# Cross attention and experts on one core: 192 key slots a batch, queries made half a period earlier, the first batch's rows on VectorE, four score banks before the first logits

## The chip, the cores and the metric

One core of one Trainium2 chip. The metric is the device time of one execution in microseconds, the median of several runs. One execution was also profiled; the rows below are of that one.

## What is computed

Eight batches of 512 tokens, width 256. Cut to what matters:

```python
x  = x + tanh(g_xattn) * xattn(layernorm(x), ctx)          # (8, 512, 256)
x  = x + tanh(g_ffn)   * experts(layernorm(x))

def xattn(q, kv):
    qp = q @ Wq.T
    idx = argmax(qp @ kv.T, -1)                 # each token picks ONE of 512 context rows
    mkv = take(kv, idx) @ Wkv.T                 # 512 picked rows, many of them the same
    mk, mv = split(mkv)                         # one head of width 16, shared by 16 query heads
    out = softmax(heads(qp) @ mk.T / 4) @ mv
    return out @ Wc.T

def experts(x):                                 # 8 experts, the best 2 of each token
    ...gelu(x @ w1[e] + b1[e]) @ w2[e] + b2[e]
```

The kernel does not attend to 512 picked rows but to the distinct ones, each with the number of tokens that picked it. It packs them into a fixed number of slots (`SLOTS`). Each batch's number of distinct rows is kept in `k.n_chosen`; where one exceeds `SLOTS`, a flag (`k.wide`) sends all engines through a second, general path that does select and attend again over 512 keys. Counted from the reference on its inputs, the eight batches pick 164, 173, 168, 148, 161, 148, 171 and 167 distinct rows.

## The kernel before

`flow` handles all batches in one software pipeline. `each_step` runs through periods `p` and 32 steps in each; every engine's program is written out in this order, and an engine keeps it strictly. In period `p` the kernel attends for batch `p` (logits, exponentials, weighted values), takes the row maxima of batch `p + 1`, selects keys for batch `s = p + 2`, and finishes batch `e = p - 1` (heads, output projection, residual, second layernorm, gate, expert queues). A table of constants (`PE_TURN_X`, `ACT_QUERY`, `DVE_QUEUE` and so on) says at which step of a period an engine issues a piece of work. No real time passes in a step that holds no work.

What is written in each period, by engine, with the names and lines of the profile:

- **TensorE.** `turn_x` (L980) turns the normalised rows at step 0, `project` (L997) makes the queries at steps 2 and 3, `keys_values` (L1007), four `scores` (L1022) at steps 5, 7, 9 and 11, `counts` (L1032) at 15, `ranks` (L1040) at 18, `pack` (L1048, L1052) at 22. One `logits_b` (L1065, two products of 256 columns) a step makes the logits from which VectorE takes row maxima; its first tile for a batch comes `MAX_EARLY` = 7 steps before the period of that work. One `logits` (L1086) a step, `weighted` (L1096) every fourth. For the batch before: `turn_heads`, `project_out` (L1121), `turn_rows`, `gates`, `rank` (L1152) at step 30.
- **VectorE.** `take_max` (L815) once a step, `best_key` (L784, L785) after each of the four scores, `x_stats` (L844), `positions` (L802 is its scan), and at steps 29 to 31 `choose`, `shares` (L900 to L906) and `queue_slots` (L911 to L918).
- **ScalarE.** `exponentials` (L677) once a step, copies out of PSUM (`turned_x`, `query`, `copy_sums` L683 at lag 11), `packed_keys` (L654).
- **GpSimd.** `chosen_keys` (L547, L548), `places` (L564), `normalise_x` (L573), `query_lo` (L541), weight remainders (L616), and `scatter` (L592), eight indirect DMAs, at step 31.
- **SyncE.** `queries` stores the split queries and loads them again in another layout; `load_x`, `load_ctx`, `load_piece` (weights).

Three banks matter for waits. Scores and `logits_b` share the two banks `ps_d` in turn; `logits` has the two banks `ps_a`, which stay unused until batch 0's first logits; `ps_r` and `ps_e` are shared by most small products. Before use, TensorE waits until the last reader of the bank is done.

```python
def max_tile(p, step):
    m, tile = divmod(p * STEPS + step + MAX_EARLY, STEPS)
    return (m + 1, tile) if is_batch(m + 1) else None
...
bank_d[n % 2].wait_read(pe)
```

After `flow`, `experts` (L2166 on) runs 39 tiles of 256 queued rows with TensorE without a break.

## Time and profile before

| | us |
|---|---|
| median of 3 runs | 1034.34 (1034.08 to 1035.05) |
| the profiled execution | 1032.27 |
| its span in the trace | 1030.5 |
| start of batch 0's first logits | 103.61 |
| starts of periods 1 to 7 | 155.2, 208.6, 265.3, 322.3, 379.3, 436.2, 481.2 |
| end of period 7 | 520.8 |
| first product of the expert tiles | 587.42 |

TensorE is busy 847.4 us of the span (82%), VectorE 546.3 (53%), GpSimd 456.3 (44%), ScalarE 410.3 (40%). How to read the rows of the timeline further down: start, length, engine, line, operation, output tile and input tiles, shape, how many instructions are merged (x8); in square brackets how long the engine had been idle before and what ended that. TensorE's instructions overlap, so what one costs is the distance between starts. A float32 product shows as two records.

### The profile page before, as it was taken

The numbers are of one execution on the slowest core, as the hardware profiler recorded it, in microseconds if no ns is written. First come the engines' busy times: TensorE is split into PE (matmuls) and PEld (weight loads), VectorE is DVE, ScalarE is ACT, GpSimd is POOL, SyncE is SP. The second block draws the span as 40 slices with busy tenths as digits, with TensorE's granted clock in tenths as the row PEclk, the third lists the DMA queues.
The fourth block names the chain that finished last, engine by engine and source line by source line (L and its number), as shares of the span: only waits on it lengthen the run. The fifth ranks groups of instructions, "written<-read, shape, count | busy, mean of one in ns | idle before, by whom it ended". The sixth has DMA issues, their size and how long they took to land. (4 is left out here: it accounts for less than half of the span.)

```text
span 1030.5 us, 20778 instructions
## 1 busy us (share of the span) xinstructions
PE 847.4 (82%) x6444; PEld 583.5 (57%) x6445; DVE 546.3 (53%) x1518; ACT 410.3 (40%) x818; POOL 456.3 (44%) x491
## 2 busy tenths in 40 slices
PE   2486889888887879787741199999999999999994
PEld 1232334444343434332230189889998898898884
DVE  2457486867686775865133144544545545445441
ACT  1120354645455453657631043433333334334330
POOL 6857263656555565443454012333423323323334
PEclk9776899989999989989975599999999999999998
DMA  4523414243342424222432422231322322322310
GB/s 154 133 91 84 87 48 92 84 123 94 101 96 94 109 68 83 83 100 83 129 102 92 131 42 43 42 50 32 56 44 41 57 43 41 60 42 41 53 14 2
DMA packets 65691, 76.40 MB, mean 74 GB/s; under 512 B 7392, under 2 KB 59360, under 8 KB 65504
## 3 DMA queue, kind: packets, MB, share of 16 engines
q1 hardware_dynamic: 51328, 58.74, 21.4%
q0 software_dynamic: 14304, 16.93, 9.3%
q8 instruction: 30, 0.49, 0.2%
q14 instruction: 29, 0.24, 0.1%
HBM read 47.68 MB, written 29.53 MB: 75 GB/s over the span
## 5 line engine op out<-in xcount | busy, mean ns | idle before, releaser
L677 ACT ACTIVATE prob<-ps_a 128x512 f32<-128x512 f32 x256 | 151.5, 602 | 190.3 <-PE ps_a L1086 184.5
L815 DVE TENSOR_REDUCE row_max<-ps_d 128x2 f32<-128x512 f32 x256 | 170.0, 682 | 85.7 <-PE ps_d L1065 78.5
L2340 PE MATMUL ps_h<-x_hi,w_split 128*128 128x256 bf16 x1248 | 212.2, 274 | 0.0
L2354 PE MATMUL ps_y<-w_split,hidden 128*128 x1248 | 206.4, 273 | 0.0
L2340 PE MATMUL ps_h<-x_lo,w_split 128*128 128x256 bf16 x624 | 170.8, 274 | 0.0
L2354 PE MATMUL ps_y<-w_split,h_lo 128*128 x624 | 170.1, 273 | 0.0
L2250 ACT ACTIVATE hidden<-ps_h,bias 128x256 f32<-128x256 f32 x312 | 130.8, 470 | 88.3 <-PE ps_h L2340 88.3
L2224 POOL DMA_INDIRECT out<-y,token_at x78 | 129.3, 1657 | 43.9 <-POOL token_at L2222 30.5
L1065 PE MATMUL ps_d<-k_st,w_split 96*128 96x256 bf16 x512 | 107.1, 296 | 32.9 <-DVE row_max L815 20.9
L2340 PEld LDWEIGHTS ps_h<-x_hi,w_split 128*128 x1248 | 122.6, 98 | 14.3
L2354 PEld LDWEIGHTS ps_y<-w_split,hidden 128*128 128x128 bf16 x1248 | 122.1, 98 | 14.1
L2220 POOL TENSOR_TENSOR token_f<-tails,ones_f 128x2 f32<-128x2 f32 x39 | 7.8, 200 | 267.2 <-DVE y L2296 266.0
L2293 DVE TENSOR_TENSOR y<-ps_y,b_all 128x512 f32<-128x512 f32 x39 | 27.0, 691 | 174.6 <-PE ps_y L2354 174.6
L2239 ACT CAST x_hi<-ps_x 128x512 bf16<-128x512 f32 x39 | 22.8, 585 | 212.1 <-PE ps_x L2327 212.1
L1086 PE MATMUL ps_a<-w_split,k_st 98*128 98x512 bf16 x256 | 100.4, 398 | 7.9 <-ACT prob L677 6.6
L2307 DVE TENSOR_TENSOR h_lo<-hidden 128x512 bf16<-128x512 f32 x156 | 99.6, 683 | 12.3 <-ACT hidden L2250 9.4
L616 POOL TENSOR_TENSOR w_split<-w_stage,w_split 128x1024 bf16<-128x1024 f32 x32 | 68.0, 2129 | 85.6 <-ACT w_split L746 85.5
L1065 PEld LDWEIGHTS ps_d<-k_st,w_split 96*128 96x128 bf16 x512 | 45.5, 102 | 101.7 <-DVE row_max L815 44.5
L1096 PE MATMUL ps_o<-prob,v_st 128*32 128x512 f32 x512 | 72.0, 636 | 0.7 <-ACT prob L677 0.7
L592 POOL DMA_INDIRECT queue<-rows,slot x64 | 62.9, 982 | 19.4 <-issue 17.1
L1086 PEld LDWEIGHTS ps_a<-w_split,k_st 98*128 98x128 bf16 x256 | 24.8, 99 | 74.3 <-ACT prob L677 48.3
L1022 PE MATMUL ps_d<-ctx_sb,q_t 128*128 128x512 f32 x128 | 62.3, 611 | 4.2 <-DVE row_max L815 3.5
(190 smaller groups left out, 1078.1 us busy)
## 6 DMA issues: line engine op xcount, KB each, us to landing
w_stage<-w SPq DMA_DIRECT2D x32, 512.0 KB, 3.4
xg<-queue SPq DMA_DIRECT2D x39, 260.0 KB
w_split<-q_split SPq DMA_DIRECT2D x24, 256.0 KB, 6.4
x_in<-x SPq DMA_DIRECT2D x8, 512.0 KB
ctx_sb<-ctx_t SPq DMA_DIRECT2D x8, 512.0 KB, 3.5
x<-x SPq DMA_DIRECT2D x8, 512.0 KB, 3.4
q_split<-q_hl SPq DMA_DIRECT2D x16, 256.0 KB, 2.3
out<-x SPq DMA_DIRECT2D x8, 512.0 KB, 3.0
```

What stands on the lines that cost most here:

```text
L592: pool.indirect_dma_start(k.queue[:], bass.IndirectOffsetOnAxis(ap=slot[:, t, c:c + 1], axis=0), rows[:, t, :], None).then_inc(scattered, 16)
L616: g.tensor_tensor(lo, stage, hi, ALU.subtract).then_inc(w_lo, 1)
L677: a.activation(prob[n % 2][:, j, :], ps_a[step % 2][:], ACT.Exp, scale=SCALE).then_inc(exp_ready, 1)
L815: v.tensor_reduce(row_max[:, t, 2 * pair:2 * pair + 2], bank.rearrange("p (h r) -> p h r", h=2), AX.X, ALU.max).then_inc(max_taken, 1)
L1065: last = t_.matmul(ps_d[n % 2][:, c * SLOTS:(c + 1) * SLOTS], q_st[m % 3][0:ROW_MAX, 2 * pair + c, t * P:(t + 1) * P], k_st[0:ROW_MAX, m % ...
L1086: t_.matmul(ps_a[step % 2][:], k_st[:, b % 3, key_tile * P:(key_tile + 1) * P], q_st[b % 3][:, QUAD * group + j, :], start=True, stop=True ...
L1096: last = t_.matmul(ps_o[j * VW:(j + 1) * VW, :], v_st[:, b % 3, key_tile, :], prob[n % 2][:, j, :], start=(key_tile == 0), stop=(key_tile ...
L2224: pool.indirect_dma_start(k.out_rows, bass.IndirectOffsetOnAxis(ap=token_at[:, t:t + 1], axis=0), y[s][:, t, :], None, bounds_check=B * L ...
L2250: last = a.activation(hidden[s][:, f, :], ps_h[n][:, c, :], ACT.Gelu, bias=bias[s][:, f:f + 1])
L2307: v.tensor_tensor(h_lo[s][:, both, :], hidden[s][:, both, :], h_hi[s][:, both, :], ALU.subtract).then_inc(h_lo_ready, 1)
L2340: last = t_.matmul(ps_h[n][:, c, :], k.w1_split[:, bass.ds(e, 1), part, kt, f].rearrange("p a f -> p (a f)"), xs[s][:, kt, :], start=(q == ...
L2354: last = t_.matmul(ps_y[s][:, t, :], hs[s][:, f, token], k.w2_split[:, bass.ds(e, 1), part, f, :].rearrange("p a d -> p (a d)"), start=(q ...
```

## The change

Seven edits, all in `flow`:

1. `SLOTS` is 192 instead of 256. `logits_b` multiplies 2 x 192 columns, `take_max` reduces 384 elements instead of 512, `places` compares with 192 columns. The second key tile holds 64 keys: for two heads at a time two products of 64 rows go to the upper and lower half of one bank, and one exponential reads both. A group of four heads has 6 banks of logits instead of 8, at steps 0, 1, 2, 3, 4 and 6 of eight (`LOGITS_AT`). `packed_keys` copies the values in three pieces, not one, and `pack` has 24 value products, not 16.
2. `turn_x` and `project` for a batch move from steps 0, 2, 3 of period `s - 2` to steps 14, 16, 17 of period `s - 3`; with them the copies on ScalarE, the remainders on GpSimd (step 24) and the store on SyncE (step 25). The reload (`stack`) stays in period `s - 2`, at step 1. Loading and normalising x move a period earlier too.
3. Batch 0's `normalise_x`, `chosen_keys` and `places` are done by VectorE; for the other batches GpSimd keeps them.
4. In periods before 0, scores and `logits_b` go round four banks (`ps_d` and `ps_a`).
5. `rank` moves from step 30 to 31, `queue_slots` and `scatter` from step 31 to step 0 of the period after.
6. `copy_sums` has lag 10, not 11.
7. New waits: `turned_x` waits for `project_out` of the batch four before, `turned_rows` for the `project` of the batch four later, since they share the tile `turned`.

```diff
-SLOTS = SLOT_TILES * P
+SLOTS = 192
...
+        FEW = SLOTS - P
+        LOGITS_AT = (0, 1, 2, 3, 4, 6)
...
-        PE_TURN_X, PE_PROJECT, PE_KV, PE_TURN_KV, PE_SCORES = 0, (2, 3), 6, 8, (5, 7, 9, 11)
+        PE_TURN_X, PE_PROJECT, PE_KV, PE_TURN_KV, PE_SCORES = 14, (16, 17), 6, 8, (5, 7, 9, 11)
...
+        def ring(p, n):
+
+            return n % 4 if p < 0 else n % 2
...
+                if s == 0:
+                    dve.wait_ge(scores_read, t + 1)
+                    chain.then(v.tensor_copy(best[:, t:t + 1], top8_at[:, t, 0:1]))
+                    v.tensor_scalar(chosen[:, t, :], column[:], best[:, t:t + 1], None, ALU.is_equal
+                                    ).then_inc(chosen_ready, 1)
...
+                if s == 0:
+                    dve.wait_ge(position_ready, 1)
+                    for t in range(LT):
+                        last = v.tensor_scalar(place[:, t, :], column[:, 0:SLOTS], position[:, t:t + 1], None, ALU.is_equal)
+                    last.then_inc(place_ready, 1)
...
+                if i < QUAD:
+                    last = t_.matmul(ps_a[i % 2][:], k_st[:, b % 3, 0:P], q_st[b % 3][:, QUAD * group + i, :],
+                                     start=True, stop=True)
+                else:
+                    for c in range(2):
+                        last = t_.matmul(ps_a[i % 2][c * FEW:(c + 1) * FEW, :], k_st[:, b % 3, P:SLOTS],
+                                         q_st[b % 3][:, QUAD * group + 2 * (i - QUAD) + c, :], start=True, stop=True)
```

What the tables move, first on TensorE before the first packing (`ps_e<-ident,x_in` is `turn_x`, `ps_e<-turned,wq_sb` `project`, `ps_r<-ones_bf,chosen` `counts`, `ps_r<-used,...` `ranks`, `ps_e<-chosen,key_cols` the start of `pack`). Before:

```order
L1022 MATMUL ps_d<-ctx_sb,q_t 128x512 x4
L1032 MATMUL ps_r<-ones_bf,chosen 128x1 x16
L1040 MATMUL ps_r<-used,before 128x4
L1041 MATMUL ps_r<-used,ones_bf 128x4
L1048 MATMUL ps_e<-chosen,key_cols 98x256 x4
```

With the change:

```order
L1064 MATMUL ps_a0<-ctx_sb,q_t 128x512 x2
L1064 MATMUL ps_a1<-ctx_sb,q_t 128x512 x2
L1022 MATMUL ps_e0<-ident,x_in 128x128 x4
L1022 MATMUL ps_e1<-ident,x_in 128x128 x4
L1074 MATMUL ps_r<-ones_bf,chosen 128x1 x16
L1039 MATMUL ps_e0<-turned,wq_sb 128x512 x2
L1039 MATMUL ps_e1<-turned,wq_sb 128x512 x2
L1082 MATMUL ps_r<-used,before 128x4
L1083 MATMUL ps_r<-used,ones_bf 128x4
L1090 MATMUL ps_e0<-chosen,key_cols 98x192 x4
```

The turn and the projection of batch 1 now stand inside batch 0's selection, the projection ahead of its ranks; the last scores use the banks `ps_a`.

Then on TensorE at the border of two periods in the middle of the run (`ps_r<-either,...` is `rank`, `ps_o<-prob,v_st` `weighted`). Before:

```order
L1086 MATMUL ps_a<-w_split,k_st 128x512
L1065 MATMUL ps_d<-k_st,w_split 128x256 x2
L1152 MATMUL ps_r<-either,before 128x32
L1153 MATMUL ps_r<-either,ones_bf 128x32
L1086 MATMUL ps_a<-w_split,k_st 128x512
L1065 MATMUL ps_d<-k_st,w_split 128x256 x2
L1086 MATMUL ps_a<-w_split,k_st 128x512
L1065 MATMUL ps_d<-k_st,w_split 128x256 x2
L980 MATMUL ps_e<-ident,x_in 128x128 x8
```

With the change:

```order
L1131 MATMUL ps_a<-w_split,k_st 64x512 x2
L1107 MATMUL ps_d<-k_st,w_split 128x192 x4
L1200 MATMUL ps_r<-either,before 128x32
L1201 MATMUL ps_r<-either,ones_bf 128x32
L1127 MATMUL ps_a<-w_split,k_st 128x512
L1107 MATMUL ps_d<-k_st,w_split 128x192 x2
L1127 MATMUL ps_a<-w_split,k_st 128x512
L1107 MATMUL ps_d<-k_st,w_split 128x192 x2
L1144 MATMUL ps_o<-prob,v_st 32x512 x4
```

`turn_x` and, behind it, the projection are gone from here; one step more of row-maximum products stands ahead of `rank`.

And on VectorE at the same border (`row_max` rows are `take_max`, `rows<-share,ratio` and `token` end `shares`, `queue_end` begins `queue_slots`). Before:

```order
L905 TENSOR_TENSOR rows<-share,ratio 128x4
L906 TENSOR_SCALAR token<-token 128x4
L911 TENSOR_TENSOR queue_end<-n_queued,queue_at 128x8
L914 TENSOR_TENSOR queue_end<-queue_end,ps_r 128x8
L915 TENSOR_TENSOR n_queued<-n_queued,ps_r 128x8
```

With the change:

```order
L946 TENSOR_TENSOR rows<-share,ratio 128x4
L947 TENSOR_SCALAR token<-token 128x4
L849 TENSOR_REDUCE row_max<-ps_d 128x2
L58 ISA
L952 TENSOR_TENSOR queue_end<-n_queued,queue_at 128x8
L955 TENSOR_TENSOR queue_end<-queue_end,ps_r 128x8
```

One row maximum stands between the two pieces now; the pieces are the same.

## Rows read from the trace of the kernel before

**Rows 1.** Page, the chain that ended last, by line.

```profile
PE ps_h L2340 20%; PE ps_y L2354 19%; PE ps_x L2327 2%; DMA xg<-queue 1%; DMA out<-y,token_at 0%; POOL out L2224 0%; DVE y L2293 0%; DVE x_lo L2285 0%; ACT x_hi L2239 0%; DVEq L2181 0%; SPq L2152 0%; SPq L2195 0%; SPq L2191 0%; DVE y L2296 0%; POOL token_f L2220 0%
```

**Rows 2.** Stretches: length; PE, PEld, DVE, ACT, POOL busy; clock, DMA share, GB/s.

```profile
103.61:155.18 51.57, 44.51 (x258) 19.59 (x259) 33.49 (x74) 24.71 (x46) 24.06 (x25) 0.91 0.29 68
...
322.34:379.32 56.98, 46.99 (x321) 23.22 (x320) 41.21 (x124) 29.94 (x57) 33.59 (x37) 1.00 0.37 98
...
436.20:481.20 45.00, 36.27 (x222) 16.00 (x220) 28.98 (x88) 27.73 (x50) 18.04 (x16) 0.89 0.31 104
481.20:520.80 39.60, 28.21 (x170) 11.03 (x170) 11.41 (x62) 27.96 (x52) 17.97 (x16) 0.96 0.34 110
520.80:576.60 55.80, 13.62 (x63) 9.38 (x63) 15.65 (x79) 8.94 (x15) 26.29 (x26) 0.57 0.32 105
```

**Rows 3.** Timeline of TensorE ahead of period 0.

```profile
49.62 1.09 PE L1048 MATMUL ps_e<-chosen,key_cols 128*98 128x256 bf16 x4 [6.95 <-POOL chosen L564]
60.23 3.75 PE L997 MATMUL ps_e<-turned,wq_sb 128*128 128x512 f32 x4 [0.40 <-ACT turned L635]
67.49 1.96 PE L1022 MATMUL ps_d<-ctx_sb,q_t 128*128 128x512 f32 x4 [0.66 <-DVE row_max L815]
94.98 1.09 PE L1048 MATMUL ps_e<-chosen,key_cols 128*98 128x256 bf16 x4 [1.59 <-POOL chosen L564]
103.61 0.61 PE L1086 MATMUL ps_a<-w_split,k_st 98*128 98x512 bf16 x1 [0.50 <-DMA w_split<-max_t]
```

**Rows 4.** Timeline of VectorE and GpSimd ahead of period 0.

```profile
9.39 1.41 DVE L844 BATCH_NORM_STATS2 stats<-x_in 128x6 f32<-128x256 f32 x4
28.81 0.70 DVE L784 MAX8 top<-ps_d 128x8 f32<-128x512 f32 x1 [17.60 <-PE ps_d L1022]
43.55 2.09 DVE L802 TENSOR_TENSOR_SCAN offset<-ones_f,total 128x4 f32<-128x4 f32 x1
...
12.79 4.83 POOL L573 TENSOR_SCALAR x_in<-x_in,moments,rstd 128x256 f32<-128x256 f32 x4
39.70 1.57 POOL L548 TENSOR_SCALAR chosen<-column,best 128x512 bf16<-128x512 f16 x1
43.50 2.12 POOL L616 TENSOR_TENSOR w_split<-w_stage,w_split 128x1024 bf16<-128x1024 f32 x1
45.94 3.62 POOL L564 TENSOR_SCALAR chosen<-column,position 128x256 bf16<-128x256 f16 x4 [0.32 <-DVE position L803]
```

**Rows 5.** Timeline of TensorE in period 4 and at its end.

```profile
325.74 0.39 PE L1065 MATMUL ps_d<-k_st,w_split 96*128 96x256 bf16 x2 [2.14 <-DVE row_max L815]
...
327.06 0.39 PE L1086 MATMUL ps_a<-w_split,k_st 98*128 98x512 bf16 x1
327.29 0.39 PE L1065 MATMUL ps_d<-k_st,w_split 96*128 96x256 bf16 x2
327.51 1.88 PE L997 MATMUL ps_e<-turned,wq_sb 128*128 128x512 f32 x4
...
357.15 0.39 PE L1086 MATMUL ps_a<-w_split,k_st 98*128 98x512 bf16 x1 [0.62 <-ACT prob L677]
361.12 0.39 PE L1065 MATMUL ps_d<-k_st,w_split 96*128 96x256 bf16 x2 [0.64 <-DVE row_max L815]
365.39 0.64 PE L1048 MATMUL ps_e<-chosen,key_cols 128*98 128x256 bf16 x4 [1.15 <-POOL chosen L564]
373.26 0.66 PE L1105 MATMUL ps_r<-ident,sums 128*128 128x128 f32 x4 [0.51 <-ACT sums L683]
377.72 0.19 PE L1152 MATMUL ps_r<-either,before 128*128 128x32 bf16 x1 [1.72 <-DVE either L896]
```

**Rows 6.** Timeline of VectorE in period 4: three row maxima in a run.

```profile
324.99 1.89 DVE L815 TENSOR_REDUCE row_max<-ps_d 128x2 f32<-128x512 f32 x3
```

**Rows 7.** Timeline of TensorE around step 1 of period 6.

```profile
441.38 1.94 PE L1096 MATMUL ps_o<-prob,v_st 128*32 128x512 f32 x8
447.48 1.07 PE L1096 MATMUL ps_o<-prob,v_st 128*32 128x512 f32 x8
```

More of the change, by code:

```diff
@@ L282, in flow @@
         max_t = sb(own, "max_t", [2 * H, L], BF16)
-        prob = [sb(own, f"prob{c}", [P, QUAD, L]) for c in range(2)]
+        prob = [sb(own, f"prob{c}", [P, QUAD // (c + 1), L]) for c in range(2)]
         sums = sb(own, "sums", [P, L])
@@ L488, in _ @@
                 m, s, e = p + 1, p + 2, p - 1
-                if step == SP_X and p > -3 and is_batch(p + 3):
-                    load_x(p + 3)
-                if step == SP_QUERIES and is_batch(s):
-                    queries(s)
+                if step == SP_X and p > -4 and is_batch(p + 4):
+                    load_x(p + 4)
+                if step == SP_QUERIES and is_batch(p + 3):
+                    queries(p + 3)
+                if step == SP_STACK and is_batch(s):
+                    stack(s)
                 if step == SP_CTX and is_batch(s) and is_batch(s + 1):
@@ L557, in values @@
                 chain.then(g.tensor_copy(value_cols[:, :, 0:V1], value_f[:]))
-                chain.step(g.tensor_tensor(value_cols[:, :, V1:2 * V1], value_f[:], value_cols[:, :, 0:V1], ALU.subtract))
+                last = g.tensor_tensor(value_cols[:, :, V1:2 * V1], value_f[:], value_cols[:, :, 0:V1], ALU.subtract)
+                if s:
+                    chain.step(last)
+                else:
+                    last.then_inc(place_ready, 1)
             def places(s):
@@ L596, in _ @@
                 s, e = p + 2, p - 1
-                if step == POOL_QUERY_LO and is_batch(s):
-                    query_lo(s)
-                for t in due(s, POOL_CHOSEN, step):
+                if step == POOL_QUERY_LO and is_batch(p + 3):
+                    query_lo(p + 3)
+                for t in (due(s, POOL_CHOSEN, step) if s else ()):
                     chosen_keys(s, t)
@@ L931, in _ @@
                 if step in DVE_BEST and is_batch(s):
-                    best_key(s, DVE_BEST.index(step), ps_d[n_d % 2][:])
+                    best_key(s, DVE_BEST.index(step), (ps_d + ps_a)[ring(p, n_d)][:])
                     n_d += 1
@@ L935, in _ @@
                     add(e, c)
-                for t in due(p + 3, DVE_X_STATS, step):
-                    x_stats(p + 3, t)
+                for t in due(p + 4, DVE_X_STATS, step):
+                    x_stats(p + 4, t)
                 for t in due(e, DVE_STATS, step):
@@ L947, in _ @@
                     shift_of(e)
[L948 to L949 removed]
+                if step == DVE_X_MOMENTS and is_batch(p + 4):
+                    x_moments_of(p + 4)
                 if step == DVE_SPLIT_MAX and is_batch(m):
@@ L957, in _ @@
                     shares(e)
-                if step == DVE_QUEUE and is_batch(e):
-                    queue_slots(e)
+                if step == DVE_QUEUE and is_batch(e - 1):
+                    queue_slots(e - 1)
                 row_tile = max_tile(p, step)
                 if row_tile:
-                    take_max(*row_tile, ps_d[n_d % 2][:])
+                    take_max(*row_tile, (ps_d + ps_a)[ring(p, n_d)][:])
                     n_d += 1
@@ L1159, in _ @@
                 if is_batch(p):
-                    logits(p, step)
+                    if step % (2 * QUAD) in LOGITS_AT:
+                        logits(p, step // (2 * QUAD), LOGITS_AT.index(step % (2 * QUAD)))
                 row_tile = max_tile(p, step)
                 if row_tile:
-                    logits_b(*row_tile, n_d)
+                    logits_b(*row_tile, ring(p, n_d))
                     n_d += 1
@@ L1170, in _ @@
                     turn_sums(*given)
-                if step == PE_TURN_X and is_batch(s):
-                    turn_x(s)
-                if step in PE_PROJECT and is_batch(s):
-                    project(s, PE_PROJECT.index(step))
+                if step == PE_TURN_X and is_batch(p + 3):
+                    turn_x(p + 3)
+                if step in PE_PROJECT and is_batch(p + 3):
+                    project(p + 3, PE_PROJECT.index(step))
                 if step == PE_KV and is_batch(s):
@@ L1181, in _ @@
                 if step in PE_SCORES and is_batch(s):
-                    scores(s, PE_SCORES.index(step), n_d)
+                    scores(s, PE_SCORES.index(step), ring(p, n_d))
                     n_d += 1
```

142 lines of the change are left out of this document (80 added, 62 removed).

## The prediction

> **What bounds the kernel now.** I read the chain that ended last first. It reaches back only to 577 us, and what stands in it is TensorE in the two layers of the experts [rows 1], a stage that the change does not touch: it gives and costs nothing, if the expert tiles merely start earlier. So the whole effect is the time at which `flow` ends. The busy time by stretch [rows 2] splits that: period 0 takes 51.6 us, period 4 57.0 (periods 2 to 5 are 56.7 to 57.0, period 1 is 53.4), period 6 45.0, period 7 39.6, then a tail of 55.8 without attention. In period 4 TensorE is busy 47.0 of 57.0 us and VectorE 41.2: TensorE bounds it, with waits on VectorE. Ahead of period 0 it is another picture: 103.6 us in which TensorE mostly waits for one serial chain through VectorE and GpSimd [rows 3, 4]. Durations are those of the profiled execution, 1032.27 us; the median of the runs is 2.1 us above it. An effect under 0.2% (2 us) could not be told from none.
>
> **Unit costs.** A row maximum over 512 elements comes every 0.60 us in a run (1.89 for three, the last one 0.69 long) [rows 6]; statistics over 256 elements come every 0.35 [rows 4]. Between them 384 elements cost 0.47. On GpSimd 512 columns take 1.57 us and 256 take 0.90 (3.62 for four) [rows 4], so 192 take 0.74. On TensorE one logits product takes 0.23 from start to start, a pair for the row maxima 0.22, that is 0.11 for 256 columns, so 0.08 for 192; half a projection takes about 1.72 (1.88 with its overlap) [rows 5].
>
> **1. Up to the first packing (49.6 us now).** Normalising batch 0 on GpSimd takes 4.83 us [rows 4]; on VectorE four instructions of 256 elements, 0.35 each by the nearest row, 1.4: the chain starts 3.4 earlier, the first `best_key` at 25.4 instead of 28.8. On VectorE each tile then costs 1.45 for maximum and index, 0.2 for the copy and at most 0.6 for the comparison, with keys and values (0.8) 9.8 us in all: the last row of batch 0 is chosen at 35.3, while GpSimd ends at 41.3 now (39.70 plus 1.57 [rows 4]). That would be 6 us. Two things take most of it back. First, the order: batch 1's projection stands ahead of batch 0's `ranks`. Its input is normalised by GpSimd only after `query_lo` of batch 0 (until 26.4), 1.3 us of deviation and 4.83: 32.6; turned and copied at about 36. The projection takes 3.4 us at the full clock and 7.1 at half (3.75 is one half of it at the low clock [rows 3]); I take 6: ranks at about 43, later than the 42.5 of now. Second, VectorE and GpSimd get in each other's way: the scan over five elements takes 2.09 us and ends at 45.64, when GpSimd's weight remainder, begun at 43.50, ends at 45.62 [rows 4]. Copies and comparisons of batch 0 on VectorE would wait so behind `query_lo`, four normalisations of 1.2 and the remainders, about 3 us in all, and positions come 3.3 us behind the ranks. The Trainium skill's page "SBUF — State Buffer" (section "SBUF: two separate sides") has the rule: GpSimd and VectorE share one pair of ports and the loser waits for the whole instruction, if VectorE reads two SBUF inputs or is in a two-port mode. By this row it holds for the scan; by the page it would also hold for VectorE's new comparisons, and for these no row exists: without it this part would be 3 us better. The place comparisons take 4 x 0.35 instead of 3.62. Sum: first packing at about 48.5, **-1**, bounds -3.5 (no collision, projection at full clock) and +2 (every new VectorE instruction waits behind one of GpSimd).
>
> **2. From there to the first logits (54.0 us now, 49.62 to 103.61).** Four parts. Up to the first scores of batch 1 (67.49 [rows 3]) TensorE has 12 tiles of row maxima with `turn_x` and a projection at the low clock in between; afterwards 12 tiles from four banks at VectorE's 0.47: 5.9 instead of 15.6, -9.7. The four scores and eight tiles took 17.4 us, each score and each maximum waiting for the other through two banks; with four, VectorE's own work is the bound, 4 x 1.45 + 8 x 0.47 + 0.8 = 10.4, and the first score runs at the low clock: 12, -5. Turn and projection of batch 2 are new at steps 14 to 17: +3.6. The places take 0.7 less, and nothing but them and positions stands between ranks and pack (94.98): -1.6. From pack to logits it is the same chain, 8.6 us. Sum -12.7, I take **-12**; bounds -18 (full clock throughout) and -5 (all of TensorE's work in it at half clock).
>
> **3. Period 0 (51.6).** Steps 0 to 4 lose turn and projection, which ran at the low clock: 12.8 us become 5.7, -7.1. The same work returns at steps 14 to 17, 2 x 1.72 + 0.9 and 0.5 of waiting for its copy, +4.9; the first scores fall to the low clock, +1.8. Products for the maxima -1.7 (64 x 0.027), waits -1.9. **-4**.
>
> **4. Periods 1 to 4.** The products give -1.7 each, where TensorE bounds. The waits at steps 15 to 18, 0.62 on an exponential, 0.28 and 0.64 on row maxima, go under the projection that now stands there: -1.5 [rows 5]. The wait of 0.51 on `copy_sums` goes with its lag: -0.5. At the border of the periods VectorE's `choose` (2.95), `shares` (1.1) and `queue_slots` (1.9) stay, only cut in two, with five row maxima 8.4 us, in which TensorE has 3.8 us of work; the waits of 1.72 and 2.14 [rows 5] are not removed but moved, and grow to about 4.5, since turn and projection no longer fill this place. Up to the start of step 3 this stretch takes 1.6 less than now, but the turn's 0.9 is paid elsewhere: -0.75. What is late next: `pack` waits for the places (1.15 now [rows 5]), about 1.6, as TensorE has less to do before: +0.45. Turn and projection at their new place wait 0.2 for `add` and 0.5 for their copy: +0.7; scores wait 0.2 more. `pack` has eight small products more, +0.1. Logits: 6 banks, but 8 products as before, four of them in pairs of 64 rows; I count them at the full 0.23 each and no gain. ScalarE's eight exponentials a period fewer (0.5 each) cost nothing and give nothing here; it is busy 29.9 of 57. `scatter` and `stack` have moved past GpSimd's and SyncE's other work; GpSimd's first `chosen_keys` comes 3 us later than VectorE's result, and catches up by the third, as each takes 1.75 and they come every 4.2. Sum **-3.0** in each of 2, 3 and 4, -2.5 in period 1; bounds -6 and 0.
>
> **5. Period 5** also loses a turn and a projection (4.3), as batch 7 is projected in period 4, and gets 1.3 of the waits back that the projection had covered: **-6**. **Period 6** (45.0): products -1.7, sums -1.6, row maxima -0.7: **-4**. **Period 7** (39.6) goes from exponential to exponential through two banks, 0.54 each: two fewer in each of four groups, -4.3; pairs +0.8; sums one exponential earlier, -2.5: **-6**. **Tail**: it hangs on GpSimd, which must end the scatter of batch 6 before the weight remainders and the last deviation; `queue_slots` and `scatter` come as soon as before, as no step with work lies in between: 0.
>
> Sum: -1 - 12 - 4 - 2.5 - 9 - 6 - 4 - 6 = **-44.5**. From the median of 1034.3 that is **990**; the profile's own time would be 988.
>
> **The rivals.** *A. Paired halves (chance 0.15).* Four products with 32 columns, 8 records, take 1.07 us together [rows 7], while two full float32 products take over 1.8 (1.96, [rows 3]): narrow products run side by side. If the 64-row pairs do, each pair takes 0.23 and not 0.46, 8 x 0.23 = 1.8 a period, 14 in all: about 976. Against it: a pair of row-maximum products just before a change to narrow ones costs 0.1 more than elsewhere, and there are eight changes a period more. The page "TensorEngine Tiling (Array Packing)" of the Trainium skill says both: up to twice as fast for 64 columns ("Theoretical Speedup"), and a drain of the array at each change of mode ("Key Properties"); by the first 976, by the second again 990. *B. VectorE bounds the border and gives nothing to the steady periods (0.13).* Then only parts 1 to 3 and the ends remain, with 4.3 in period 5: -1 - 12 - 4 - 4.3 - 2 - 4 = -27, 1007. For it: the waits of 1.72 and 2.14 grow. *C. The lead loses more (0.12).* The lock and the projection ahead of the ranks cost what the four banks give: parts 1 and 2 together -4, 999. *D. The clock (0.04), slower.* At the border TensorE now idles over half of 8.4 us with no projection behind it. In period 6, which already is so, `weighted` takes 1.94 at 441.4 and 1.07 again at 447.5 [rows 7]: the clock fell to half (1.2 GHz) and came back within 6 us. Should it stay low in periods 1 to 5 through steps 30 to 13, some 18 us of work would double: +90 against -44.5, 1080. It decides from 9 us a period on; period 6 speaks against it, with at most 3. *E. The change doesn't do what it says (0.01):* a batch with more than 192 rows would send all through the general path, select and attend again, +400 (the length of periods 0 to 7). The largest count is 173.
>
> **How the numbers follow.** Forecast 0.55, A 0.15, B 0.13, C 0.12, D 0.04, E 0.01. The forecast's own bounds with A's below and B's above give 974 to 1008, which leaves out D, E and the ends of A and B, under 0.2. Faster by over 0.2%: 0.93, as A, B, C and the forecast all are, less what I may have missed; the same 0.02; slower 0.05.
>
> **What would show it.** First logits at about 90.5 (now 103.6), first packing near 48.5, batch 1's projection before it. Row maxima 0.47 apart in a run. Period 0 near 47.5, periods 2 to 4 near 54, 5 near 51, 6 near 41, 7 near 33.5; end of period 7 near 476, tail still 56. Waits on `row_max` at steps 1 and 2 of 1 to 2 us each, none at 15 to 18. I am wrong if the first packing comes after 52, if periods 2 to 4 are still 57, or if `weighted` in steps 29 to 9 of the middle periods takes 1.9.

## The result and the profile after

The changed kernel takes 994.03 us (median of 4 runs, 993.29 to 994.43), the kernel before 1034.62 beside it: ratio 0.9612, 95% interval 0.9596 to 0.9628. That is 40.6 us, where 44.5 were forecast; 994 lies inside 974 to 1008. The profiled execution took 994.43 us, its span is 992.7 us. Runs more than 1.5% above the fastest of their kernel are left out of the ratios further down, but not of the medians and ranges: two of `border_undone`, one of `all_three`. The sum came out nearly right, its parts did not. `rank` is issued once near the end of each period from 1 on, so its starts cut the run into comparable pieces:

| stretch | before | after | difference | forecast |
|---|---|---|---|---|
| start of the span to first packing | 49.62 | 52.90 | +3.3 | -1 |
| first packing to first logits | 53.99 | 47.07 | -6.9 | -12 |
| first logits to first `rank` (periods 0, 1) | 103.41 | 94.76 | -8.7 | -6.5 |
| next three (periods 2, 3, 4) | 56.88, 57.02, 56.80 | 55.88, 52.08, 54.91 | -1.0, -4.9, -1.9 | -3 each |
| period 5 | 58.30 | 49.99 | -8.3 | -6 |
| period 6 | 45.06 | 36.42 | -8.6 | -4 |
| period 7 | 38.56 | 35.41 | -3.2 | -6 |
| to the last `rank` | 33.54 | 33.83 | +0.3 | 0 |
| to the first product of the expert tiles | 34.24 | 35.76 | +1.5 | 0 |

The page of after, the chain that ended last, by line. It is the chain of [rows 1], link by link; the two largest shares are a point higher, of a span that is 37.8 us shorter:

```profile
PE ps_h L2389 21%; PE ps_y L2403 20%; PE ps_x L2376 2%; DMA xg<-queue 1%; DMA out<-y,token_at 0%; POOL out L2273 0%; DVE y L2342 0%; DVE x_lo L2334 0%; ACT x_hi L2288 0%; DVEq L2230 0%; SPq L2201 0%; SPq L2244 0%; SPq L2240 0%; DVE y L2345 0%; POOL token_f L2269 0%
```

So the whole difference is again when the expert tiles start: 549.01 instead of 587.42 us.

Timeline of TensorE after, the lead (`ps_e<-chosen,key_cols` starts a packing, L1127 is batch 0's first logits):

```profile
52.90 0.87 PE L1090 MATMUL ps_e<-chosen,key_cols 128*98 128x192 bf16 x4 [9.53 <-DVE chosen L836]
55.71 0.80 PE L1107 MATMUL ps_d<-k_st,w_split 96*128 96x192 bf16 x4 [0.95 <-issue]
61.11 3.75 PE L1064 MATMUL ps_d<-ctx_sb,q_t 128*128 128x512 f32 x4
73.78 1.04 PE L1022 MATMUL ps_e<-ident,x_in 128*128 128x128 f32 x8
78.47 0.56 PE L1074 MATMUL ps_r<-ones_bf,chosen 128*128 128x1 bf16 x16 [3.12 <-POOL chosen L559]
79.17 3.41 PE L1039 MATMUL ps_e<-turned,wq_sb 128*128 128x512 f32 x4
91.27 0.88 PE L1090 MATMUL ps_e<-chosen,key_cols 128*98 128x192 bf16 x4 [5.62 <-POOL chosen L579]
99.97 0.61 PE L1127 MATMUL ps_a<-w_split,k_st 98*128 98x512 bf16 x1 [2.14 <-DMA w_split<-max_t]
```

Timeline of VectorE ahead of the first packing:

```profile
38.51 1.15 DVE L821 TENSOR_SCALAR used<-count 128x4 bf16<-128x4 f32 x1
...
50.84 0.43 DVE L878 BATCH_NORM_STATS2 stats<-x_in 128x6 f32<-128x256 f32 x1 [10.98 <-DMA x_in<-x]
51.37 0.16 DVE L828 TENSOR_TENSOR position<-ps_r,unused 128x4 f32<-128x4 f32 x1
...
52.04 0.81 DVE L836 TENSOR_SCALAR chosen<-column,position 128x192 bf16<-128x192 f16 x4
```

Two things are to be seen. Up to the first packing VectorE stands idle for 10.98 us, not for batch 0's ranks, which had been ready since 43.4, but for a load of x that batch 2 needs: its first statistics stand at step 18, and `positions` of batch 0 at step 19 behind them. From 55.71 to 73.78 the second selection goes nearly as forecast (5.4 us to the first scores and 12.7 through them, forecast 5.9 and 12). Then it takes 17.5 to the second packing, with 3.12 and 5.62 us of waiting for GpSimd; my terms give 12.1 there (10.1 before, +3.6, -1.6).

The stretches between `rank`s after (length; PE, PEld, DVE, ACT, POOL busy; clock, DMA share, GB/s):

```profile
194.73:250.61 55.88, 50.52 (x328) 24.58 (x327) 37.55 (x123) 25.57 (x50) 33.05 (x37) 0.88 0.39 100
250.61:302.69 52.08, 46.12 (x329) 22.53 (x327) 37.34 (x123) 25.27 (x50) 32.83 (x37) 0.97 0.42 108
302.69:357.60 54.91, 49.02 (x329) 23.59 (x328) 36.06 (x115) 25.38 (x50) 26.81 (x31) 0.91 0.38 92
357.60:407.59 49.99, 43.10 (x312) 20.80 (x311) 36.56 (x117) 22.79 (x45) 24.69 (x30) 0.92 0.35 83
407.59:444.01 36.42, 31.94 (x219) 14.68 (x216) 24.52 (x87) 23.16 (x42) 18.02 (x16) 0.92 0.36 114
444.01:479.42 35.41, 28.42 (x163) 11.37 (x164) 10.58 (x57) 23.10 (x43) 17.95 (x16) 0.86 0.37 120
```

The first three hold the same work and differ by 3.8 us; the longer, the lower the granted clock (0.88, 0.91, 0.97). Before, the same three stood at 0.94, 0.97 and 1.00 and were alike to 0.2 us, so there the low clock cost nothing. TensorE behind the border, after:

```profile
194.56 0.34 PE L1107 MATMUL ps_d<-k_st,w_split 96*128 96x192 bf16 x2 [2.56 <-DVE row_max L849]
194.73 0.18 PE L1200 MATMUL ps_r<-either,before 128*128 128x32 bf16 x1
...
196.58 0.50 PE L1107 MATMUL ps_d<-k_st,w_split 96*128 96x192 bf16 x2 [0.46 <-DVE row_max L849]
197.01 1.94 PE L1144 MATMUL ps_o<-prob,v_st 128*32 128x512 f32 x8
...
202.66 1.94 PE L1144 MATMUL ps_o<-prob,v_st 128*32 128x512 f32 x8
```

`weighted` takes 1.94, as in the first of [rows 7]: the clock has fallen to 1.2 GHz, the lower of its two levels, and `weighted` is at it still at 202.66. In the middle stretch only one `weighted` is so. The first stretch has a second time at 1.2 GHz, from 239 to 243 in the middle of its period, with no wait over 0.46 us just before it. VectorE and GpSimd in the wait at the border, after:

```profile
192.12 1.27 DVE L931 TENSOR_TENSOR gap<-top 128x4 f32<-128x4 f32 x1
...
193.51 0.17 DVE L934 COPY rows<-choice 128x4 f32<-128x4 f32 x1
```

```profile
191.25 2.12 POOL L635 TENSOR_TENSOR w_split<-w_stage,w_split 128x1024 bf16<-128x1024 f32 x1
```

A subtraction of four columns takes 1.27 us and ends with GpSimd's instruction; a copy of as many takes 0.17.

### The profile page after: what moved, and what is told of

It reads as the page before. It is cut to its first block and busy times, and to the rows that moved or that the text cites. A ratio compares the mean times of both kernels' runs of the same rounds, so it can differ in the third digit from the quotient of the medians.

```text
span 992.7 us, 20863 instructions
## 1 busy us (share of the span) xinstructions
PE 832.3 (84%) x6508; PEld 579.8 (58%) x6509; DVE 517.9 (52%) x1534; ACT 376.7 (38%) x770; POOL 438.1 (44%) x475
## 5 line engine op out<-in xcount | busy, mean ns | idle before, releaser
L698 ACT ACTIVATE prob<-ps_a 128x512 f32<-128x512 f32 x192 | 113.0, 603 | 181.5 <-PE ps_a L1127 108.2
L849 DVE TENSOR_REDUCE row_max<-ps_d 128x2 f32<-128x384 f32 x237 | 127.9, 551 | 60.8 <-PE ps_d L1107 59.2
L1107 PE MATMUL ps_d<-k_st,w_split 96*128 96x192 bf16 x474 | 84.5, 268 | 25.7 <-DVE row_max L849 19.2
L1107 PEld LDWEIGHTS ps_d<-k_st,w_split 96*128 96x128 bf16 x474 | 40.0, 103 | 77.6 <-DVE row_max L849 32.0
L1144 PE MATMUL ps_o<-prob,v_st 128*32 128x512 f32 x512 | 77.1, 678 | 3.0 <-ACT prob L698 3.0
L2389 PEld LDWEIGHTS ps_h<-x_lo,w_split 128*128 x624 | 61.4, 98 | 7.4
L2403 PEld LDWEIGHTS ps_y<-w_split,h_lo 128*128 128x128 bf16 x624 | 61.1, 98 | 7.1
L1064 PE MATMUL ps_d<-ctx_sb,q_t 128*128 128x512 f32 x112 | 57.8, 640 | 2.2 <-DVE row_max L849 1.4
```

The source lines that it names most:

```text
L698: a.activation(prob[n % 2][:, j, :], ps_a[i % 2][:], ACT.Exp, scale=SCALE).then_inc(exp_ready, 1)
L849: v.tensor_reduce(row_max[:, t, 2 * pair:2 * pair + 2], bank[:, 0:2 * SLOTS].rearrange("p (h r) -> p h r", h=2), AX.X, ALU.max).then_inc(m ...
L1064: last = t_.matmul(ps_da[n][:], q_t[:, kt, t * P:(t + 1) * P], ctx_sb[:, kt, :], start=(kt == 0), stop=(kt == KT - 1))
L1107: last = t_.matmul(ps_da[n][:, c * SLOTS:(c + 1) * SLOTS], q_st[m % 3][0:ROW_MAX, 2 * pair + c, t * P:(t + 1) * P], k_st[0:ROW_MAX, m % 3, ...
L1144: last = t_.matmul(ps_o[j * VW:(j + 1) * VW, :], values, probs, start=(key_tile == 0), stop=(key_tile == SLOT_TILES - 1))
L2389: last = t_.matmul(ps_h[n][:, c, :], k.w1_split[:, bass.ds(e, 1), part, kt, f].rearrange("p a f -> p (a f)"), xs[s][:, kt, :], start=(q == ...
```

## The experiments

Medians in us; a difference between two of these kernels is uncertain by about 3 us, and by 4 to 6 where one of them is `filler`, `all_three` or `border_undone`, whose runs spread more. "Pack" and "logits" are the starts of the first packing and of batch 0's first logits in the profiled execution.

| kernel | median (lowest to highest) | ratio to before, 95% | pack | logits |
|---|---|---|---|---|
| the change | 994.03 (993.29 to 994.43) | 0.9596 to 0.9628 | 52.90 | 99.97 |
| `slots_only` | 1011.86 (1009.52 to 1017.69) | 0.9765 to 0.9823 | 51.48 | 102.98 |
| `stats_after` | 986.74 (985.84 to 988.10) | 0.9534 to 0.9574 | 45.19 | 93.66 |
| `rows_pool` | 1004.38 (1001.92 to 1004.89) | 0.9688 to 0.9732 | 62.83 | 109.89 |
| `two_banks` | 993.20 (990.16 to 996.00) | 0.9583 to 0.9627 | 51.48 | 103.41 |
| `banks_late` | 991.88 (988.73 to 993.93) | 0.9560 to 0.9611 | 47.31 | 101.81 |
| `project_late` | 971.54 (970.46 to 976.61) | 0.9387 to 0.9437 | 46.64 | 88.53 |
| `border_undone` | 1002.38 (994.82 to 1014.72) | 0.9621 to 0.9728 | 50.19 | 98.08 |
| `sums_late` | 1003.70 (999.83 to 1005.21) | 0.9688 to 0.9737 | 51.02 | 97.62 |
| `weights_moved` | 982.05 (979.73 to 983.90) | 0.9482 to 0.9527 | 49.80 | 96.81 |
| `filler` | 983.11 (981.18 to 994.33) | 0.9493 to 0.9569 | 53.85 | 100.79 |
| `best` | 976.00 (973.70 to 977.00) | 0.9419 to 0.9462 | 45.02 | 91.01 |
| `all_three` | 973.51 (966.60 to 983.96) | 0.9372 to 0.9446 | 46.60 | 89.29 |

**The slots alone.** All places that edit 1 touches, in the kernel before:

```diff
-SLOTS = SLOT_TILES * P
+SLOTS = 192
```

> Edit: the kernel before with 192 slots alone (edit 1); turn and projection, banks, batch 0's rows, `rank`, `queue_slots` and `copy_sums` as before. Theory (my terms of the sum, with the pairs of 64 rows at the 0.34 that the change's trace shows): row maxima of the lead -3, period 0 -2, periods 1 to 5 -2 each, period 6 -2.5, period 7 -4: about -21, 1013, ratio 0.980. Rival 1 (the moves make room for it, alone it goes into waits on row maxima and exponentials): -10, 1024, ratio 0.990. Rival 2 (nearly all of the gain is this edit): -33 or more, 1001, ratio below 0.97.

1011.86, 22 us under before: the theory's 21. Its profiled execution took 1015.10. Between its `rank`s it takes 54.97, 54.80, 56.32, 54.69, 43.47 and 37.42. The edit is worth half of the change, and 1.9, 2.2 and 0.5 us in the middle periods; against this kernel the moves took 2.7 and 1.4 off two of the middle periods and added 0.9 to one, and took 4.7 and 7.1 off periods 5 and 6.

**The load of x.**

```diff
-DVE_X_STATS, DVE_X_MOMENTS = (18, 22, 22, 23), 24
+DVE_X_STATS, DVE_X_MOMENTS = (20, 22, 22, 23), 24
```

> Edit: the first tile of the x statistics goes from step 18 to step 20, behind `positions` on VectorE. Theory (the load of x): in the change, VectorE stands 10.98 us in front of this tile while the ranks of batch 0 are ready behind it; without that, the first packing comes at 45 to 46 us instead of 52.9, the first logits at about 92.5 instead of 99.97, and the time is 986 to 987 (ratio to before 0.954). Rival 1 (projection and ports, as I forecast them): the chain of ranks, positions and places is itself not ready before about 50; first packing 50 or later, time 991 to 993. Rival 2: the gain is taken back by the first logits, which wait for loads anyway: 993 to 994.

986.74. TensorE of this kernel:

```profile
36.84 6.74 PE L1039 MATMUL ps_e<-turned,wq_sb 128*128 128x512 f32 x8
43.42 0.17 PE L1082 MATMUL ps_r<-used,before 128*128 128x4 bf16 x1
...
45.19 0.53 PE L1090 MATMUL ps_e<-chosen,key_cols 128*98 128x192 bf16 x4 [1.57 <-DVE chosen L836]
```

The packing comes 1.8 us behind the ranks, and 6.3 of the 7.7 gained there reach the first logits. Another 2.7 come in the first middle stretch (53.22 us, with one `weighted` at the low clock instead of two, and no second fall in the middle of the period), and 0.6 are lost in periods 0 and 1. One number of a step in a table cost the change 7 us.

**Batch 0's rows (edit 3).** The copy, comparison, places and normalisation of batch 0 go back to GpSimd, with their semaphores; the diff is shortened:

```diff
-for t in (due(s, POOL_CHOSEN, step) if s else ()):
+for t in due(s, POOL_CHOSEN, step):
...
-if step == POOL_PLACE and is_batch(s) and s:
+if step == POOL_PLACE and is_batch(s):
...
```

> Edit 3 undone alone: batch 0's normalisation, chosen keys and places on GpSimd again. Theory (VectorE waits for the load of x at the same place, and that load hangs on the store and reload of batch 0's queries, which come 3.4 us later): first packing at 58 to 59 instead of 52.9 (3 from the later load, 2.8 from the places), time about 999. Rival 1 (all of it lies beside the wait for the load, but for the places): +3, 997. Rival 2 (GpSimd without these pieces helped only itself): 994.

1004.38, more than forecast. GpSimd of this kernel:

```profile
48.08 1.58 POOL L559 TENSOR_SCALAR chosen<-column,best 128x512 bf16<-128x512 f16 x1
...
57.68 2.12 POOL L629 TENSOR_TENSOR w_split<-w_stage,w_split 128x1024 bf16<-128x1024 f32 x1 [5.75 <-ACT w_split L764]
59.78 2.99 POOL L576 TENSOR_SCALAR chosen<-column,position 128x192 bf16<-128x192 f16 x4
```

Batch 0's last keys are chosen at 49.7 instead of 37.6, so the load of x (landed by 53.1) no longer decides alone, and the places stand behind a weight remainder that waits for ScalarE. Edit 3 is worth 10 us here; I had put -1 on all of part 1. But 49.7 is also 8.4 later than in the kernel before (41.3), since GpSimd now normalises batch 1 (33.41 to 38.26) ahead of batch 0's chosen keys: in part edit 3 pays back what edit 2 costs. Edit 2 was not undone by itself in any run, so its own worth stays open. The edits that were measured alone, 22 us for the slots, 10 for this one, 5 for the four banks and 10 for the sums (both below), already come to more than the 40.6 of the whole; whether they add isn't shown.

**The four banks (edit 4)**, first on the change, then on `stats_after`:

```diff
-return n % 4 if p < 0 else n % 2
+return n % 2
```

> Edit: in the periods before 0 scores and row-maximum logits go round two banks again, not four. Theory (my forecast of 5 us for the four banks): first packing unchanged at 52.9, first logits at 105, time 998 to 999. Rival: the lead goes at the pace of VectorE and GpSimd, and two banks do as well: 994 to 995.

> Two banks again in the periods before 0, as in `two_banks`, now with the x statistics behind `positions`, so that the load of x no longer sets the start. Theory (the four banks are worth what their stretch shows): first packing at 45.2 as in `stats_after`, first logits 4.9 later, at 98.5, and 991 to 992 against 986.7. Rival (the later steps take it back, as the time of `two_banks` suggests, equal to the change's): 986 to 988.

In the stretch itself both agree: from first packing to first logits 51.93 instead of 47.07 with the early statistics, 54.50 instead of 48.47 with the late ones, so 4.9 and 6.0 us. The total shows it only in `banks_late` (+5.1 by the medians, +3.3 by the ratios). In `two_banks` it is gone: its load of x landed sooner, its packing came 1.4 us earlier, and the first stretch between `rank`s took 53.3 us, not 55.9, with one `weighted` at the low clock instead of two. The theory holds for the stretch; my expectation for the total of `two_banks` was a miss.

**The projection ahead of the ranks**, on `stats_after`:

```diff
-PE_TURN_X, PE_PROJECT, PE_KV, PE_TURN_KV, PE_SCORES = 14, (16, 17), 6, 8, (5, 7, 9, 11)
+PE_TURN_X, PE_PROJECT, PE_KV, PE_TURN_KV, PE_SCORES = 14, (19, 20), 6, 8, (5, 7, 9, 11)
-ACT_TURNED_X, ACT_QUERY, ACT_QUERY_HI, ACT_PACKED = 15, (17, 18), 20, 23
+ACT_TURNED_X, ACT_QUERY, ACT_QUERY_HI, ACT_PACKED = 15, (20, 21), 21, 23
```

> With the x statistics at step 20: the projection of the batch three ahead at steps 19 and 20 instead of 16 and 17, behind `ranks`. Theory (my reason of part 1: in the lead the projection of batch 1 holds batch 0's ranks up by about 5 us): first packing at 40 to 42 instead of 45.2, first logits 3 to 4 earlier, 983. The waits at steps 15 to 18 that the projection covered come back in the steady periods, +0.5 a period at most. Rival 1 (the queries stored later delay their reload, and with it the row maxima of batch 1): lead unchanged, 987. Rival 2 (steady periods lose more than the lead gains): 989 or more.

971.54, 15 us under `stats_after`, far more than any theory said. The first packing did not come earlier but 1.5 us later. The ranks do come earlier, at 40.54 instead of 43.42, so the projection had held them up; but the packing then waits for the copies of the projection, whose banks it shares, and so stands behind it either way. What gains is the second selection, 41.9 us from packing to logits instead of 48.5. GpSimd in `stats_after`:

```profile
79.85 2.13 POOL L635 TENSOR_TENSOR w_split<-w_stage,w_split 128x1024 bf16<-128x1024 f32 x1 [5.89 <-ACT w_split L770]
81.95 3.00 POOL L579 TENSOR_SCALAR chosen<-column,position 128x192 bf16<-128x192 f16 x4
```

and in `project_late`:

```profile
74.75 2.12 POOL L635 TENSOR_TENSOR w_split<-w_stage,w_split 128x1024 bf16<-128x1024 f32 x1
77.19 2.99 POOL L579 TENSOR_SCALAR chosen<-column,position 128x192 bf16<-128x192 f16 x4 [0.32 <-DVE position L832]
```

The places of batch 1 stand behind a remainder, the remainder waits for ScalarE's cast at step 18, and that stood behind the copies of the projection at 17 and 18. With the copies at 20 and 21 this chain through four engines is broken. Another 2.6 us come from periods 0 and 1, and 5.8 from the middle of the run, stretches of 51.59, 51.42 and 51.41 instead of 53.22, 52.14 and 54.83, with a clock of 0.94 to 0.97 instead of 0.91 to 0.95: the next runs are about that.

**The clock at the border.** On the change, products whose results nobody reads, where TensorE waits:

```diff
+def fill(b, many):
+    bank_a[0].wait_read(pe)
+    for i in range(many):
+        t_.matmul(ps_a[0][:], k_st[0:ROW_MAX, (b + 1) % 3, 0:P], q_st[(b + 1) % 3][0:ROW_MAX, i, :], start=True, stop=True)
...
+if step == 31 and 1 <= p < B - 1:
+    fill(p, 10)
```

> Edit: the changed kernel with ten more products of 128x512, whose results nobody reads, into the free bank `ps_a[0]` at step 31 of periods 1 to 6, where TensorE waits 1.0 to 2.6 us for a row maximum. Theory (the clock at the border): the granted clock falls to 1.2 GHz at the border because TensorE waits there; with the wait filled, `weighted` behind the border takes 1.06 instead of 1.94, and the two periods of 55.9 and 54.9 us come down to 52 to 53: 6 us less in all, 988. Rival (the clock falls for other reasons, or the fill only delays the row maxima): the dips stay, time 994 to 998.

983.11: the kernel does 60 more products and is 11 us faster (one of its six runs took 994). TensorE at the border of 194.56 above:

```profile
192.63 2.32 PE L1103 MATMUL ps_a<-w_split,k_st 96*128 96x512 bf16 x10
195.37 0.34 PE L1112 MATMUL ps_d<-k_st,w_split 96*128 96x192 bf16 x2 [0.41 <-DVE row_max L849]
...
197.66 1.06 PE L1149 MATMUL ps_o<-prob,v_st 128*32 128x512 f32 x8
```

and its stretches:

```profile
195.54:247.06 51.52, 46.95 (x338) 23.12 (x337) 37.21 (x123) 25.45 (x50) 32.98 (x37) 1.00 0.43 108
247.06:298.56 51.50, 46.94 (x338) 23.11 (x337) 37.23 (x123) 25.45 (x50) 32.82 (x37) 1.00 0.44 110
298.56:349.99 51.43, 46.95 (x338) 23.13 (x337) 35.65 (x115) 25.45 (x50) 26.76 (x31) 1.00 0.40 98
349.99:400.44 50.45, 45.60 (x323) 21.46 (x322) 36.48 (x117) 22.85 (x45) 24.70 (x30) 0.93 0.35 81
400.44:437.44 37.00, 31.93 (x229) 14.95 (x228) 25.48 (x92) 23.24 (x42) 18.02 (x16) 1.00 0.37 122
437.44:468.65 31.21, 24.69 (x164) 10.21 (x163) 9.63 (x50) 22.99 (x43) 17.97 (x16) 1.00 0.38 126
```

The three middle stretches are now alike to 0.1 us at the full clock. The low clock had cost 4.4, 0.6 and 3.5 us in them: in the change and in `stats_after` a stretch with one `weighted` at the low clock is 0.6 to 1.7 us longer than these, one with two 3.4 to 3.5. Why the clock comes back after one at some borders and after two at others isn't settled. The filled wait did not do it everywhere: behind the border of period 5 the clock fell all the same (0.93, 0.5 us longer than in the change), and period 6 is 0.6 longer although it is at 1.00 (0.92 in the change). Period 7 is 4.2 shorter, but only its beginning is filled. TensorE in it, in the change and in `filler`:

```profile
465.17 1.93 PE L1144 MATMUL ps_o<-prob,v_st 128*32 128x512 f32 x8 [2.35 <-ACT prob L698]
```

```profile
457.52 1.07 PE L1149 MATMUL ps_o<-prob,v_st 128*32 128x512 f32 x8 [1.41 <-ACT prob L698]
```

The wait is shorter since a cast on ScalarE, ahead of the exponential, waits 0.53 us for a weight load and not 1.47. That gives 1.1 of the 4.2; the other 3.1 come behind it, where the clock has fallen in the change and not here. So part of the 11 us hangs on when a load lands. Between the runs of one kernel time and granted clock go together, too: `border_undone` took 995 at a mean clock of 0.92 in three runs and 1009 at 0.90 in another, `all_three` 967 and 968 at 0.93 and 980 at 0.91. Which of the two moves the other is not shown by that.

**GpSimd beside the border.**

```diff
-W_TWO = (14, 28)
+W_TWO = (6, 14)
```

> Edit: in periods with two weight pieces GpSimd's remainders stand at steps 6 and 14 instead of 14 and 28, so that none runs while VectorE makes `choose`, `shares` and `queue_slots`. Theory (GpSimd and VectorE hold each other up): `gap` takes 0.14 instead of 1.27 us, the wait of TensorE behind the border shrinks by about 1 us in each of periods 1 to 5, and the time is about 989 (ratio 0.956). Rival (the border waits for something else, such as the row maxima themselves): under 1 us in all, 993 to 994.5.

982.05, twice the gain expected. VectorE and TensorE of this kernel:

```profile
188.96 0.14 DVE L931 TENSOR_TENSOR gap<-top 128x4 f32<-128x4 f32 x1
```

```profile
190.33 0.34 PE L1107 MATMUL ps_d<-k_st,w_split 96*128 96x192 bf16 x2 [1.50 <-DVE row_max L849]
```

`gap` is down from 1.27 to 0.14 and the wait from 2.56 to 1.50, as the theory has it. In the change `gap` ends at 193.39, with GpSimd's remainder (from 191.25, 2.12 long). The stretches are 53.79, 51.26, 51.27, 49.60, 38.58 and 34.26: four shorter by 2.1, 0.8, 3.6 and 0.4, period 6 longer by 2.2 (two `weighted` low), period 7 shorter by 1.1. Periods 0 and 1, which end behind a border, are 1.1 shorter. The rest came ahead of the first logits (3.2, a load of x that landed earlier) and in the tail (1.3). So some 7 of the 12 go with the edit: about 1 a border by the shorter wait, while the clock gave in one place (0.97 instead of 0.91 in the stretch that gained 3.6) and took in another (0.87 instead of 0.92 in period 6). That load set the first packing anywhere from 49.8 to 53.9 in five kernels written alike up to there; the cause of that spread stays open.

**The border uncut (edit 5)**, `scatter` on GpSimd in the same way:

```diff
-PE_RANK = 31
+PE_RANK = 30
-if step == DVE_QUEUE and is_batch(e - 1):      # DVE_QUEUE = 0
-    queue_slots(e - 1)
+if step == DVE_QUEUE and is_batch(e):          # DVE_QUEUE = 31
+    queue_slots(e)
```

> Edit 5 undone alone: `rank` at step 30, `queue_slots` and `scatter` at step 31 of the same period. Theory (the cut helps, since one row maximum more comes to TensorE before the long piece on VectorE): waits behind `rank` grow by about 1 us a period, time 999. Rival 1 (VectorE has the same work there and bounds the border either way): 993 to 995. Rival 2: the whole border is better uncut, 990.

Open by the time: 995 in three runs, 1009 to 1015 in the others, and the interval of the ratio overlaps with the change's. Its profiled execution, of 995, has waits of 2.12 and 2.95 us at the border, where the change has 2.56 and 0.46 to 1.00, middle stretches of 54.20, 54.37 and 54.37 (162.9 together, the change 162.9), 51.21 in period 5 (+1.2) and 39.43 in period 6 (+3.0). In the middle periods the cut gives nothing in sum: the waits are 1.7 to 2.3 us shorter a border, but two stretches of the change have a second `weighted` at the low clock, and these none. It pays in period 6.

**The sums (edit 6).**

```diff
-ACT_SUMS, ACT_HEADS, ACT_ROWS, ACT_ROWS_T, ACT_RATIO = 10, 9, (21, 21, 22, 22), 25, 30
+ACT_SUMS, ACT_HEADS, ACT_ROWS, ACT_ROWS_T, ACT_RATIO = 11, 9, (21, 21, 22, 22), 25, 30
```

> Edit 6 undone alone: `copy_sums` at lag 11. Theory (my terms: 0.5 in each of periods 1 to 5, 1.6 in period 6, 2.5 in period 7): period 7 is 2.5 us longer, all in all +4 to +6, 998 to 1000. Rival (in the last periods the exponentials alone set the pace, and the copy hides): 994 to 995.

1003.70, above the expected 998 to 1000: edit 6 is worth 10 us by the medians, about twice what I had. Its profiled execution is its fastest, at 999.83; there periods 0 and 1 are 1.5 us longer, periods 5, 6 and 7 by 2.7, 2.6 and 2.3, and the middle ones take 162.7, no more than in the change. A row of its period 7:

```profile
469.77 0.48 PE L1153 MATMUL ps_r<-ident,sums 128*128 128x128 f32 x1 [2.17 <-ACT sums L704]
```

**Together.** `best` is `stats_after` and `weights_moved`, with the remainders of the lead at 4, 14, 20, 26; `all_three` has the late projection too.

> The x statistics behind `positions` (step 20), GpSimd's remainders at steps 6 and 14 in periods with two weight pieces, and in the period before period 0 at 4, 14, 20, 26 instead of 4, 10, 18, 26. If the gains measured alone (7.3 and 12 us against the changed kernel) add up, 974 to 976; a further 2 us if the remainders ahead of chosen keys and places (2.12 each) no longer stand in their way before the first logits: 972. Rival: the two gains share the lead's 3 us, so 978.

> The x statistics at step 20, the projection at steps 19 and 20, and the weight remainders moved as in `best`. By the sum of the single gains (7.3 for the statistics, 15.2 for the projection behind `ranks`, 12 for the weights in periods with two pieces) 959 to 960. By the rows, the middle periods of `project_late` are already down at 51.4 and those of `weights_moved` at 51.3, so that the two take the same time away: left are about 2 in the lead, 1 in period 5 and 1 in the tail, 967 to 968. Rival: the weights collide with something in the lead, 971 or more.

`best` is at the sum, 976.00. `all_three` is at 973.51 (971.88 without the slow run), where 967 to 968 were expected, with runs from 966.60 to 983.96; its fastest is the fastest of all, its median is not below that of `project_late`. In the middle periods the two edits take the same time away, as expected (51.27 to 51.48, after 51.41 to 51.59 in `project_late`). `project_late`, three lines of the table away from the change, has the lowest median: 971.54, ratio 0.9412 (0.9387 to 0.9437), 2.3% under the change.

## Why the prediction was right, and where it was not

**The bound.** Right: the experts are untouched and the gain is when they start.

**Part 1, -1: came +3.3.** The failed step is the list of what stands behind what. I walked TensorE's order (the projection ahead of `ranks`) and the sharing of ports, and not VectorE's: `x_stats` for batch 2 ahead of `positions`, waiting for a load that SyncE issued at 42.33 behind the reload of batch 0's queries. Of the two reasons that I did give, the projection was right: I had the ranks at about 43, they came at 43.18, and once it stood behind them (`project_late`) they came 2.9 earlier than in `stats_after`. The other, 3 us of instructions held up by GpSimd, was wrong: without the load the packing comes 1.8 behind the ranks, where I had 5.5, at 45.19 and so before even my lower bound of 46.1. Of the collisions one showed (`used`, 1.15 us), hidden beside the projection; the scan took 0.17 instead of 2.09, the new comparisons 0.35 to 0.50 beside a busy GpSimd. The first maximum of batch 0's scores came at 27.82 and not at 25.4, since its statistics began 1.2 later than before (10.60 instead of 9.39) and its projection took 7.0 instead of 5.7 up to the scores; that cost nothing, as the projection of batch 1 set the ranks.

**Part 2, -12: came -6.9.** Right in these terms: the tiles up to the first scores (5.4, forecast 5.9), the scores and tiles through four banks (12.7, forecast 12), from pack to logits 8.7 (8.6); what the banks are worth by `two_banks` and `banks_late` (4.9 to 6.0) fits the 5 that I had. The failed terms are "+3.6" for turn and projection and "-1.6" for the places: 17.5 us instead of 12.1, because GpSimd's remainders, one of them hung on the projection through ScalarE, stood ahead of the last chosen keys and of the places. `best`, with two of them moved, takes 12.0 there.

**Part 3 and period 1, -6.5: came -8.7.** Size only.

**Periods 2 to 4, -9: came -7.8**, but as -1.0, -4.9, -1.9. That this is near -9 is luck, for two errors met. The terms were too small for a period at the full clock: `filler`, whose products hide in the wait, takes 51.5, 5.4 under before, and not 3.0. One of them had the wrong sign: I let the waits behind the border grow from 3.9 to about 4.5, and they came to 3.0 to 3.6. The other error is the clock. I kept it out of the sum and gave it to rival D, with 0.04, all or nothing: 18 us of work at half speed or none. It was neither. The clock fell at the borders behind periods 1 to 5 and came back within 6 to 12 us, which cost up to 3.5 in a middle period, and 4.4 in the one in which it fell a second time. In the kernel before it had fallen at such borders too (0.94, 0.97 and 0.91 in the stretches behind periods 1, 2 and 4), without a cost in periods 2 and 3, and I had looked at period 6 alone. The page "SBUF — State Buffer" of the Trainium skill (section "SBUF: two separate sides"), which I applied to the lead, mattered at the border: `gap`, with two inputs in SBUF, waits for a GpSimd instruction to end (1.27 against 0.14), and the trace agrees with the rule. I had sized `choose` from its total and not asked what was in it.

**Period 5, -6: came -8.3; period 6, -4: came -8.6.** In period 6, 1.6 come from the slots, and by the two undone edits 3.0 from the border and 2.6 from the sums. I had -1.7 and -0.7, nothing for the border, and -1.6.

**Period 7, -6: came -3.2.** The sums gave 2.3 (forecast 2.5), and the clock fell to 0.86 there (0.96 before): `filler`, at 31.21 and a clock of 1.00, is 4.2 under the change (3.1 behind the fall of the clock, 1.1 by the shorter wait) and 7.4 under before, more than forecast. **Tail, 0: came +1.8.**

**The rivals.** A: a pair of 64 rows costs 0.34, between my 0.46 and the rival's 0.23. B and C each described part of what happened, but not as a whole. C had -4 for parts 1 and 2 together, and -3.6 came where the forecast had -13: in the lead the rival was right by its number, though not by its reason (the load of x and the remainders, not the lock). B's steady periods without gain did not come. E did not occur.

**What I had said would show it.** "I am wrong if the first packing comes after 52": it came at 52.90, and the part of the sum was wrong. "Or if `weighted` in steps 29 to 9 of the middle periods takes 1.9": it did. Two of three alarms rang. The total held by luck, because the 9.4 us too little in the lead, and 5.9 in the middle periods, period 7 and the tail, met 9.1 too much in periods 0 and 1, 5 and 6. That makes 38.4 in the traces; the medians are 40.6 apart, as the profiled execution of before lay 2 us under its median.

## What to carry to other kernels

Before costing a moved piece of work, write down for every engine what now stands ahead of the instruction that the next stage waits for, loads for later batches and weight pieces included: here the step of one piece was worth 7 us and that of another 15. Where an engine's clock depends on what it did before, waits are not worth what they last: cutting one by 1.1 us went with up to 3.6 less in a period, and filling it with useless products with up to 4.4 less. A total can be right for wrong reasons; stretches cut at the same instruction before and after tell.
